# GNN kernel: each 128-edge chunk scatters into its own window of 128 targets, and the next pair's second layer goes ahead of the following pair's transposes

## The reference, cut to what matters

```python
m = jnp.concatenate([x[row], x[col]], axis=1)        # row = src, col = dst
m = jax.nn.relu(m @ Wm1 + bm1)
m = jax.nn.relu(m @ Wm2 + bm2)
m_sum = jax.ops.segment_sum(m, row, num_segments=x.shape[0])
```

## Time and profile before

| | us |
|---|---|
| median of 3 runs | 911.99 (909.75 to 913.79) |
| the profiled execution | 920.58, of which the span 918.7 |
| TensorE busy in the span | 851.9 (93%) |
| the edge loop | about 142 to 510 of the span |
| ordinary pair of the loop | 5.11 to 5.12 |

### The profile page before, as it was taken

How to read it: one execution, slowest core, us unless ns; L and a number is a source line. 1 busy time by engine, 2 the same in 40 slices (tenths; PEclk the granted TensorE clock), 3 DMA queues, 4 the chain that set the end, 5 groups by cost and what they waited for, 6 DMA issues and landing times.

```text
span 918.7 us, 18692 instructions
## 1 busy us (share of the span) xinstructions
PE 851.9 (93%) x5480; PEld 545.4 (59%) x5514; DVE 662.7 (72%) x1786; ACT 503.2 (55%) x1009; POOL 292.2 (32%) x403
## 2 busy tenths in 40 slices
PE   8899949999999999999999898899899998899898
PEld 3657728989898989898889645322242223232244
DVE  6999985767766767777677466977587776877651
ACT  6432114666656666666666674566656665566531
POOL 8040047556555556555555200012031110111000
PEclk9999979999999999999999999999999999999999
DMA  3020041121212121212122100000000000000310
GB/s 87 32 87 1 0 139 60 54 69 46 69 51 70 51 69 51 68 53 70 46 71 54 47 1 1 0 1 1 1 0 1 1 1 0 1 1 0 128 57 23
DMA packets 19145, 35.87 MB, mean 39 GB/s; under 512 B 5280, under 2 KB 11552, under 8 KB 18976
## 3 DMA queue, kind: packets, MB, share of 16 engines
q0 software_dynamic: 7104, 19.41, 7.5%
q1 hardware_dynamic: 12000, 15.95, 5.1%
HBM read 29.56 MB, written 5.79 MB: 38 GB/s over the span
## 4 chain that ended last, share of the span: by engine, by line
PE 77%; DVE 15%; ACT 4%; issue 3%; POOL 1%; DMA 0%; DVEq 0%; ACTq 0%; POOLq 0%
PE PS L1453 9%; PE PS L1309 8%; PE PS L1223 7%; PE PS L1222 7%; PE PS L1170 5%; PE PS L1438 5%; PE PS L1303 5%; PE PS L1241 5%; DVE OHd L1005 5%; PE PS L1444 4%; PE PS L1215 3%; PE PS L1353 3%; PE PS L1228 3%; PE PS L1404 2%; PE PS L1300 2%
## 5 line engine op out<-in xcount | busy, mean ns | idle before, releaser
L406 POOL DMA_INDIRECT room<-Qtab,gidx x148 | 148.3, 1002 | 96.0 <-DVE gidx L837 61.2
L556 ACT ACTIVATE OHe<-OHs,sew 128x128 bf16<-128x128 bf16 x408 | 126.7, 390 | 46.6 <-DVE OHs L947 26.2
L1005 DVE CUSTOM_DVE_ANT_0 OHd<-PS,room 128x1024 bf16<-128x1024 f32 x96 | 112.3, 1220 | 8.6 <-PE PS L1404 8.5
L420 POOL TENSOR_SCALAR KV<-room,pid 128x256 bf16<-128x256 uint8 x74 | 74.9, 1012 | 134.5 <-DVE MS L912 128.8
L567 ACT ACTIVATE m2s<-m2s 128x512 f32<-128x512 f32 x68 | 42.9, 631 | 88.2 <-DVE m2s L938 60.3
L458 POOL TENSOR_TENSOR zl<-AL,Sx 128x8 f32<-128x8 f32 x9 | 1.9, 215 | 265.1 <-DVE Sx L1005 265.1
L1222 PE MATMUL PS<-Wm,m1T 128*128 128x256 f32 x276 | 83.2, 383 | 0.0
L1223 PE MATMUL PS<-Wm,m1T 128*128 128x256 f32 x276 | 82.8, 382 | 0.0
L952 DVE TENSOR_SCALAR OHd<-iotaN,dstf 128x1024 bf16<-128x1024 f16 x136 | 74.3, 586 | 9.3 <-PE PS L1309 9.3
L912 DVE TENSOR_TENSOR MS<-PS,room 128x512 f32<-128x512 f32 x68 | 47.1, 692 | 43.1 <-PE PS L1241 42.8
L938 DVE TENSOR_TENSOR m2s<-PS,bm 128x512 f32<-128x512 f32 x68 | 47.0, 691 | 42.7 <-PE PS L1223 42.7
(11 more groups left out here) (357 smaller groups left out, 1734.4 us busy)
## 6 DMA issues: line engine op xcount, KB each, us to landing
BT<-Wtab SPq DMA_DIRECT2D x1, 4096.0 KB, 13.1
room<-Qtab,gidx POOLq DMA_INDIRECT x148
room<-Stab SPq DMA_DIRECT2D x1, 2048.0 KB
Wtab<-H SPq DMA_DIRECT2D x4, 512.0 KB, 3.8
Wtab<-cs SPq DMA_DIRECT2D x4, 512.0 KB, 3.4
Qtab<-room SPq DMA_DIRECT2D x1, 1024.0 KB, 4.4
Wn<-in_L_gnn_Wn SPq DMA_DIRECT2D x1, 1024.0 KB, 5.4
x<-in_x SPq DMA_DIRECT2D x1, 512.0 KB, 4.0
```

The lines of the kernel that those rows point to most:

```text
L406: g.indirect_dma_start(out=G[:, p % SLOTS, k, :], out_offset=None, in_=Qtab, in_offset=bass.IndirectOffsetOnAxis(ap=gidx[:, p, k:k + 1], a ...
L556: a.activation(OHe[:, k, j, :], OHs[:, k, :], ACT.Copy, scale=sew[:, j, bass.ds(2 * g + k, 1)])
L1005: v.tensor_tensor_reduce(junk[n % 2], bank(4, 2), mask[:, i, :], 1.0, 2 * FAR, ALU.subtract, ALU.max, Sx[:, i, hd:hd + 1]).then_inc(S("gat ...
```

## The change

- `rngi` is made in another way. DVE masks the target numbers of each chunk (`rngp`, `sew0`), TensorE transposes them (four transposes), DVE takes the largest and smallest target of each chunk, and some 19 small instructions on tiles of 72 x 2 work out, for each chunk, a window start `place` in steps of 32 targets that doesn't cross a PSUM bank. Where a chunk doesn't fit its window of 128 (`wide`), both windows of the pair start at the pair's first block of 128 and are stepped over as many blocks as the pair touches. The result is transposed to one row (`packed_across`) and the source block is added. TensorE waits for `packed` before `sources(0, 0)`.
- The scatter's inner turn has 8 matmuls: chunk 0 at `d`, chunk 1 at `d + further`, 128 targets each; the loop runs once for a pair whose chunks fit.
- In `layers(g)` the second layer stands ahead of the wait for `msg_ready` and the transposes. On ACT the relu of the next m1T stands ahead of the relu of the second layer.
- The wait for `spans` stands ahead of the loop.

```diff
-            v.tensor_copy(paired(dstf), sdst)
-            link(v.tensor_scalar(paired(skey), sdst, 7, None, ALU.arith_shift_right))
-            link(v.tensor_copy(sew0[:], skey[:]))
-            link(v.scalar_tensor_tensor(rngp[:], sew0[:], 1.0, valid[:], ALU.add, ALU.mult))
-            v.tensor_tensor(inblk, rngp[:].unsqueeze(1).to_broadcast([P, NB, NCH]), ...
+            link(v.tensor_copy(paired(dstf), sdst))
+            v.scalar_tensor_tensor(rngp[:], dstf[:], 1.0, valid[:], ALU.add, ALU.mult)
+            v.scalar_tensor_tensor(sew0[:], dstf[:], float(-N), valid[:], ALU.add, ALU.mult)\
+                .then_inc(S("ends_marked"), 1)
...
+            v.tensor_reduce(above[:], ends[:, 0], AX.X, ALU.max)
+            v.tensor_reduce(below[:], ends[:, 1], AX.X, ALU.min).then_inc(S("ends_read"), 1)
+            eng.wait_ge(S("ends_read"), 1)
+            link(v.tensor_scalar(least[:], below[:], float(N), float(N - 1), ALU.add, ALU.min))
...
+            v.scalar_tensor_tensor(packed[:], below[:, 1:2], float(NB), below[:, 0:1], ALU.mult, ALU.add)\
+                .then_inc(S("packed"), 1)
...
+            for u, end in enumerate((rngp, sew0)):
                 for k in range(2):
+                    at = (2 * u + k) * P
+                    last = t.transpose(bank(6)[0:NPAIR, at:at + P], paired(end)[:, :, k], ident[:])
+            last.then_inc(S("ends_across"), 1)
...
-            eng.wait_ge(S("blocks_read"), 1)
+            eng.wait_ge(S("ends_read"), 1)
+            eng.wait_ge(S("packed"), 1)
+            t.transpose(bank(4)[0:1, 0:NPAIR], packed[:], ident[0:NPAIR, 0:NPAIR]).then_inc(S("packed_across"), 1)
...
                 eng.wait_ge(S("m1_ready"), g + 1)
+                second_layer(0)
+                second_layer(1).then_inc(S("m2_done"), 1)
                 eng.wait_ge(S("msg_ready"), g + 2)
                 transposes()
-                second_layer(0)
-                second_layer(1).then_inc(S("m2_done"), 1)
...
-                    least, past = eng.snap((span >> 3) & 7), eng.snap((span & 7) + 1)
+                    near = eng.snap((span << 2) & (N - STEP))
+                    past = eng.snap(near + ((span & (NB - 1)) << 7) + P)
+                    further = eng.snap(((span >> 3) & (N - STEP)) - near)
...
-                    with eng.Fori(least, past, 2) as d:
+                    with eng.Fori(near, past, P) as d:
                         for k in range(2):
-                            for i in range(2):
-                                at = d * P + i * P
-                                dst = OHd[:, k, bass.ds(at, P)]
-                                t.matmul(PS[:, bass.ds(at, P)], OHc[:, k, :], dst,
+                            at = nc.s_assert_within(d if k == 0 else d + further, 0, N - P,
+                                                    skip_runtime_bounds_check_because="windows lie inside the nodes")
+                            dst = OHd[:, k, bass.ds(at, P)]
+                            t.matmul(PS[:, bass.ds(at, P)], OHc[:, k, :], dst,
+                                     start=False, stop=False, skip_group_check=True)
+                            for j in range(3):
+                                t.matmul(PS[:, bass.ds(at + 2 * BANK, P)], OHe[:, k, j, :], dst,
                                          start=False, stop=False, skip_group_check=True)
```

On ACT, in the loop:

```diff
                     scaled_onehots(g)
+                    eng.wait_ge(S("t_done"), g + 2)
+                    a.activation(m1T[:].rearrange("p k e -> p (k e)"), bank(6), ACT.Relu).then_inc(S("m1_ready"), 1)
                     eng.wait_ge(S("m2_biased"), g + 1)
                     a.activation(m2s[:], m2s[:], ACT.Relu).then_inc(S("m2_ready"), 1)
-
-                    eng.wait_ge(S("t_done"), g + 2)
-                    a.activation(m1T[:].rearrange("p k e -> p (k e)"), bank(6), ACT.Relu).then_inc(S("m1_ready"), 1)
```

More of the change, by code:

```diff
@@ L156, in gnn_kernel @@
         FEW = 32
[L157 to L162, removed]
+        above = sb("above", [NPAIR, 2])
+        below = sb("below", [NPAIR, 2])
+        least = sb("least", [NPAIR, 2], i32)
+        steps = sb("steps", [NPAIR, 2], i32)
+        upper = sb("upper", [NPAIR, 2], i32)
+        place = sb("place", [NPAIR, 2])
+        other = sb("other", [NPAIR, 2])
+        wide = sb("wide", [NPAIR, 1])
+        packed = sb("packed", [NPAIR, 1])
+        rngi = sb("rngi", [1, NPAIR], i32)
         Wn1 = sb("Wn1", [P, 4, 4 * D])
@@ L868, in _ @@
             made = bank(5).rearrange("p (k f) -> p k f", k=2)
[L869 to L877, removed]
-                    eng.wait_ge(S("blocks_read"), 1)
-                else:
-                    link(last)
-                link(v.tensor_reduce(rngf[:, i, :], flags.rearrange("p b g -> p g b"), AX.X, ALU.max))
+            eng.wait_ge(S("ends_across"), 1)
@@ new lines, in _ @@
+            ends = bank(6)[0:NPAIR, :].rearrange("p (u k e) -> p u k e", u=2, k=2)
+            v.tensor_reduce(above[:], ends[:, 0], AX.X, ALU.max)
+            v.tensor_reduce(below[:], ends[:, 1], AX.X, ALU.min).then_inc(S("ends_read"), 1)
+            eng.wait_ge(S("ends_read"), 1)
+            link(v.tensor_scalar(least[:], below[:], float(N), float(N - 1), ALU.add, ALU.min))
+            v.tensor_scalar(steps[:], least[:], 5, None, ALU.arith_shift_right)
+            link(v.tensor_scalar(upper[:], least[:], 9, None, ALU.arith_shift_right))
@@ new lines, in _ @@
+            link(v.tensor_scalar(other[:], upper[:], float(BANK // STEP), float((BANK - P) // STEP), ALU.mult, ALU.add))
+            link(v.tensor_tensor(place[:], steps[:], other[:], ALU.min))
+            link(v.scalar_tensor_tensor(other[:], place[:], float(-STEP), above[:], ALU.mult, ALU.add))
+            link(v.tensor_tensor(wide[:], other[:, 0:1], other[:, 1:2], ALU.max))
+            v.tensor_scalar(wide[:], wide[:], float(P), None, ALU.is_gt)
+            link(v.tensor_tensor(upper[:, 0:1], least[:, 0:1], least[:, 1:2], ALU.min))
@@ new lines, in _ @@
+            link(v.tensor_scalar(upper[:, 1:2], upper[:, 0:1], 7, None, ALU.arith_shift_right))
+            link(v.tensor_tensor(above[:, 0:1], above[:, 0:1], above[:, 1:2], ALU.max))
+            link(v.scalar_tensor_tensor(above[:, 1:2], upper[:, 1:2], float(-P), above[:, 0:1], ALU.mult, ALU.add))
+            link(v.tensor_scalar(steps[:, 0:1], above[:, 1:2], float(P - 1), None, ALU.add))
+            link(v.tensor_scalar(steps[:, 1:2], steps[:, 0:1], 7, None, ALU.arith_shift_right))
+            v.scalar_tensor_tensor(below[:, 0:1], steps[:, 1:2], -1.0, wide[:], ALU.add, ALU.mult)
@@ new lines, in _ @@
+            link(v.scalar_tensor_tensor(other[:], upper[:, 1:2].to_broadcast([NPAIR, 2]), float(P // STEP), place[:],
+                                        ALU.mult, ALU.subtract))
+            link(v.scalar_tensor_tensor(place[:], other[:], wide[:, 0:1], place[:], ALU.mult, ALU.add))
+            link(v.scalar_tensor_tensor(below[:, 1:2], place[:, 1:2], float(PLACES), place[:, 0:1], ALU.mult, ALU.add))
+            v.scalar_tensor_tensor(packed[:], below[:, 1:2], float(NB), below[:, 0:1], ALU.mult, ALU.add)\
+                .then_inc(S("packed"), 1)
```

42 lines of the change are left out of this document (9 added, 33 removed).

## The result

The changed kernel takes 916.9 us (median of 8 runs, 916.2 to 921.7) and the kernel before, on the same chips, 912.2 (8 runs): a ratio of 1.0062, 95% interval 1.0045 to 1.0080. It is slower by 0.6%. The profiled execution took 916.6, with a span of 914.8 at a mean granted clock of 0.986. The forecast was 899, the range 886 to 911, with 0.08 on slower.

The account below looks back on a forecast made before the run. TensorE was taken to bound the edge loop, 5.12 us a pair falling to 4.85. Terms -13.5 - 1.2 + 6.1 + 0.6 - 3.4 - 1.8 = -13.2 took 920.6 to 907.4, scaled from the 912.0 median to 899; range 886 to 911.

Parts of the forecast that it names:

- The three loops: Three loops of dependence in an ordinary pair, (a), (b) and (c); whichever is longest was taken as the period.
- the fourth: TensorE's control instructions in a pair: forecast about 0.2 to 0.3 us shorter, with the message sum behind them 4.85 us.
- (c): Second layer's end, bias on DVE, relu on ACT, message sum: forecast to give 0.37 us, to about 4.75 a pair.
- (b): From ranks through sources, DVE's message and one-hots to the next ranks: 5.12 us before, forecast between 4.79 and 5.12.
- register arithmetic: Address blocks in the scatter's inner turn on TensorE: four instead of six, -0.28 us; splitting `span` adds 0.1.
- (a): TensorE's own work in an ordinary pair: half the scatter matmuls save 0.45 us, forecast 4.67 us.
- The rival of the late hand-over: DVE's message starts as late after TensorE's sources as before: period 5.05 us, kernel about 911 us; chance 0.18.
- Pairs with more turns: Pairs whose scatter turns again: seven at 5.99 us (+6.1), one at 7.13 (+0.6), two back to 4.85 (-3.4).
- the sum, -13.2: All forecast terms added on the profiled execution, in us: 920.6 to 907.4.
- Block ends: Eight pairs at the ends of blocks and their successors: -0.15 us each, -1.2 in all.
- the control one: Inner loop on TensorE's stream: each chunk's address costs as much as before, +8.5 us, kernel slower at 920; chance 0.09.
- Ahead of the loop: Before the edge loop, the second layer starts when pair 1's sources end: -1.8 us, with the chain for `packed` covered.

## Why the prediction was wrong

**The three loops were right, the fourth was mis-sized.** An ordinary pair of before is bound by TensorE's own work, 5.00 us: it has no idle time there. Right behind stands the second layer's way (c): it gives 4.94, with half the weight matmuls and with the windows in the old order, where the message sum waits for the relu. The change takes 8 matmuls from the one and 0.4 us from the other, as forecast (it also adds 0.05 to TensorE's own work, by the run with the order alone), and what is left is loop (b) at 4.76 (the shorter pairs of after) and the control stream. The step that failed is the one headed register arithmetic: "I take four blocks: -0.28". The address blocks did go from six to four, but two separate operations for the second window came with them, the loop's end got a 110 ns block, the split of `span` is 161 to 167 ns instead of 151, and at the head of the pair, by the wait for the ranks to be read, two operations stand 0.21 to 0.29 apart that stood 0.12 apart. From the first operation of the inner loop to its branch it is 1.54 us in the records, 1.48 before. The -0.28 was +0.06, and "control 0.2 to 0.3 shorter" was about 0.1 longer at the branch: 4.07 us into the pair against 3.97 (medians). With the windows and the old order the branch is at 3.97 too, so most of that tenth, the gap at the head, comes with the new order. A control bound that isn't shortened leaves a mean pair at 4.99, hardly under 5.04. That control is what holds it there is shown by the two runs without further turns: alike but for 0.3 us of loop control, they differ by about 10 us, while half the weight matmuls are worth nothing.

**The coupling wasn't seen.** In the trace of after the closing ranks come 0.31 us behind the pair's first control instruction in one pair and 0.07 ahead of it in the next. As I read it, a late branch makes the message sum and the ranks late; then TensorE starts the next pair behind its control, its sources are late and with them the one-hots, but control has time again. So pairs of about 5.15 and 4.80 alternate, and the mean lies above what loops (a), (b) and (c) need each. No run isolates this.

**The base.** The sum went by 5.12 us a pair, with a loop (b) that closed exactly. That was a property of that execution, or of its chip: the message followed the sources up to 0.33 later than elsewhere, and on a second trace the pair is 5.00, bound by TensorE. The prediction did note 920.6 against a median of 912.0, but scaled it away instead of asking which rows made the 0.9%. With 5.00 as base the forecast of 4.85 would have been worth 7.5 us, not 13.5. The terms given for loop (a) add up to 5.06, too, not to the 5.12 from which its 4.67 was taken. The rival of the late hand-over plays no part in the result: in after the message follows the sources by 1.12 us in 57 of the 68 pairs, though the period is near that rival's.

**Pairs with more turns:** the mean of the seven two-turn pairs is 6.28, forecast 5.99, and the triple one 7.72, forecast 7.13. A second turn costs 1.29, not 1.14, on a pair of 4.99. The pair behind the triple turn takes 6.73, which the sum didn't have. Together +9.8 where +3.3 stood. This 6.5 and the 10.9 us missing from the ordinary pairs are 17.4 of the 18.7 us between the sum, -13.2, and the account, +5.5. The number of turns was right: 462 weight matmuls. The turns and the ordinary pairs are both needed for the sign: with a single turn everywhere the kernel is at 0.9935.

**Block ends:** +1.6 instead of -1.2.

**The rival that came true** is the control one, with its mechanism and place; its point of decision, an ordinary pair that gets less than 0.17 us shorter, was right too (it got 0.05 shorter). It had a chance of 0.09 because of two address blocks that were counted without what came in their stead. Its 920 was on the base of 912 with no gain ahead of the loop; with that gain it is 918, near the 916.9 measured. That it is so near is in part luck: its price for the turns, +8.5, was under the 9.8 that they and the pair behind the triple turn cost, and it had neither the -2.6 of the ordinary pairs nor the +1.6 of the block ends.

**Ahead of the loop** the step held: the ranks of pair 0 come at 137.82 against 140.02, -2.2 where -1.8 stood, with pair 0's sources at 129.31 against 129.27. In other executions these sources start anywhere from 127.6 to 132.9, so single traces say little about absolute times there; but from them to the first ranks it is 10.75 to 10.88 us in all traces of the old preparation and order and 7.2 to 8.6 in all of the new. The chain is covered: `packed` is ready at 128.13, and the sources go at 129.31 when POOL's one-hot is there.
```profile
127.98 0.15 DVE L894 SCALAR_TENSOR_TENSOR packed<-below 72x1 f32<-72x1 f32 x1
...
129.31 1.44 PE L1241 MATMUL PS<-SKT,KV 128*128 128x256 bf16 x6 [0.76 <-POOL KV L426]
...
137.82 0.22 PE L1228 MATMUL PS<-OHs,beforeb 128*128 128x128 bf16 x1
```

## What to carry to other kernels

When a loop's control instructions end just before the work that they release, price every operation of the new address arithmetic and of the loop's own end before counting on fewer matmuls: here operations of 0.1 us each on the sequencer outweighed matmuls of 0.056 us. And look at the pairs that leave the common path: moving the first turn out of the loop gave more in the eight pairs with further turns than in the 51 with one. Where several loops of dependence stand close together (5.00 and 4.94 us here, with control between), single edits can each be worth nothing, and the pieces must be tried together: the windows alone lose, the order alone gives nothing, the first turn outside alone gives 0.3%, all three give 1.1%. And a profiled execution that stands off the median is to be explained by its rows, not scaled.

## What the hardware showed

- On one of the chips the start of a DVE instruction that waits for TensorE's sources comes about 0.4 us later than on four others (1.50 to 1.53 us after the start of the sources in the pairs shown, against 1.12), in part of the pairs, at the same granted clock of 1.00 in the loop; the kernel before takes 922 us there and 911 to 912 elsewhere. Why is open.
- A loop that turns once, with its bound at a fixed distance from its start, costs 0.3 us less on TensorE's sequencer than one whose distance is read at run time (0.22 against 0.53 us from the last address block to the branch).
- Register operations on TensorE's sequencer start about 0.1 us apart for a single one and 0.10 to 0.22 for a fused block (42 to 110 ns long); a taken branch takes 0.21 to 0.22 us, one not taken 0.07 to 0.08.
- A block of eleven control operations queued behind matmuls that waited began only when they did (402.88 behind 402.86), and the matmuls behind it started only after its end at 404.19, though what they wait for was there at 403.80.
